# First attention pass: destination scores as a column per node tile, fetched by TensorE

## The reference

```python
h_trans = features @ W_att_w.T + W_att_b
a_src, a_dst = (a[:out_dim], a[out_dim:])
logits = leaky(h_trans[src] @ a_src + h_trans[dst] @ a_dst)
exp_l = jnp.exp(logits)
denom = jax.ops.segment_sum(exp_l, dst, num_segments=num_nodes)
alpha = exp_l / (denom[dst] + 1e-09)
h_msg = features @ W1_w.T + W1_b
h_neigh = jax.ops.segment_sum(alpha * h_msg[src], dst, num_segments=num_nodes)
```

## Time and profile before

| | us |
|---|---|
| three runs, median (lowest to highest) | 6943.19 (6922.86 to 6951.63) |
| profiled execution, span from its first to its last instruction | 5685.5 |
| busy in the span: PE, PEld | 3113.8, 2734.5 |
| busy in the span: DVE, ACT, POOL | 3263.6, 1491.5, 3958.0 |
| broadcast of 256 KB in the second pass, from issue to landing | 3.4 |

### The profile page before, as it was taken

One profiled execution on the slowest core, in us unless ns is written; L12 is line 12 of the kernel. 1 busy time (PEld: TensorE's weight loads), 2 busy tenths in 40 slices (PEclk: granted clock), 3 DMA queues, 4 the chain that ended last, 5 costly groups with the idle time before them and its releaser, 6 DMA issues. The chain is left out here.

```text
span 5685.5 us, 82572 instructions
## 1 busy us (share of the span) xinstructions
PE 3113.8 (55%) x17051; PEld 2734.5 (48%) x17052; DVE 3263.6 (57%) x12090; ACT 1491.5 (26%) x5626; POOL 3958.0 (70%) x4054
## 2 busy tenths in 40 slices
PE   4444444356666666778898988433333443333333
PEld 3333333345555555657777776333333343333332
DVE  6888887676787787744444444433444443344445
ACT  2333333345555555532222223100000000000001
POOL 3777777736777777367777772677777757777774
PEclk7555555568888777865555556666666666666666
DMA  5111112214444444222121110111111121111112
GB/s 123 52 52 52 52 52 56 49 52 131 132 132 131 130 131 131 70 54 56 52 56 51 53 52 21 56 52 51 51 51 51 51 61 52 51 51 51 51 51 57
DMA packets 222234, 385.68 MB, mean 68 GB/s; under 512 B 85452, under 2 KB 121882, under 8 KB 221998
## 3 DMA queue, kind: packets, MB, share of 16 engines
q0 software_dynamic: 142944, 296.35, 19.0%
q1 hardware_dynamic: 79054, 86.72, 5.0%
HBM read 356.23 MB, written 26.56 MB: 67 GB/s over the span
## 5 line engine op out<-in xcount | busy, mean ns | idle before, releaser
L2246 POOL DMA_INDIRECT arena<-table_gcn,idx_now x1568 | 1532.2, 977 | 642.9 <-issue 422.1
L2296 PE MATMUL pair<-arena,hotf 128*128 x3328 | 726.6, 408 | 1224.7 <-POOLq L1819 1199.3
L2296 PEld LDWEIGHTS pair<-arena,hotf 128*128 128x128 f32 x3328 | 691.2, 317 | 1256.1 <-issue 1255.8
L664 POOL DMA_INDIRECT arena<-table_attention,idx_now x832 | 825.7, 992 | 272.7 <-issue 197.2
L664 POOL DMA_INDIRECT arena<-table_key_value,idx_now x832 | 789.2, 949 | 275.9 <-issue 221.1
L1852 POOL DMA_INDIRECT arena<-table_edge_mlp,idx_now x784 | 768.1, 980 | 261.2 <-issue 212.4
L2323 DVE TENSOR_TENSOR acc<-acc,pair 128x1024 f32 x208 | 253.9, 1221 | 1133.9 <-PE pair L2299 1133.9
L1069 PE MATMUL pair<-wide,hotf 128*128 128x130 f32 x1664 | 431.0, 439 | 653.3 <-ACT wide L1033 653.3
L1069 PEld LDWEIGHTS pair<-wide,hotf 128*128 128x128 f32 x1664 | 369.0, 326 | 718.5 <-ACT wide L1033 718.5
L2256 ACT COPY idx_now<-src_t 128x8 int32 (+1 forms) x204 | 39.3, 197 | 1815.2 <-PE pair L2299 1803.2
L1406 PE MATMUL pair<-wide,hotf 128*128 128x132 f32 x1664 | 314.1, 347 | 232.9 <-DVE acc L1436 232.8
(11 more groups left out here) (371 smaller groups left out, 5709.7 us busy)
## 6 DMA issues: line engine op xcount, KB each, us to landing
key<-rel_dram SPq DMA_DIRECT2D x104, 256.0 KB, 3.4
arena<-rel_dram SPq DMA_DIRECT2D x52, 512.0 KB, 3.7
arena<-table_gcn,idx_now POOLq DMA_INDIRECT x1568, 2.5
arena<-table_attention,idx_now POOLq DMA_INDIRECT x832
arena<-table_key_value,idx_now POOLq DMA_INDIRECT x832
arena<-table_edge_mlp,idx_now POOLq DMA_INDIRECT x784, 2.4
table_attention<-arena SPq DMA_DIRECT2D x13, 512.0 KB, 3.0
table_gcn<-acc SPq DMA_DIRECT2D x26, 256.0 KB, 2.3
```

Source lines behind the costliest of these rows:

```text
L664: q_.indirect_dma_start(ring[:, slot, 0:width], None, table, bass.IndirectOffsetOnAxis(ap=idx_now[:, slot:slot + 1].bitcast(U32), axis=0)) ...
L2246: q_.indirect_dma_start(conv_ring[:, slot * D:(slot + 1) * D], None, table, bass.IndirectOffsetOnAxis(ap=idx_now[:, slot:slot + 1].bitcast ...
L2296: t_.matmul(window[:, bass.ds(offset * D, D)], hot8[:, g % 2, u, :], conv_ring[:, bass.ds(slot * D, D)], start=False, stop=False)
```

## The change

The destination scores become one column per node tile. `w0` gets the score weights as one more column, so the table's projection gives the destination score of each node in column 130, and ACT copies it into `dst_score`, 128 nodes by 52 tiles. `score` on PE, its bank and the spread copy go. At the start of the pass DVE splits the scores into three 16-bit parts (`split_scores`), whose sum is the 32-bit score.

Per group, SP's broadcasts of two groups at a time bring `rel1_dram` to all partitions; DVE makes the turned one-hot of 128x512 in 16 bits (`turned_hot`), two groups ahead; PE multiplies each step's turned one-hot with the three parts of the column of that step's node tile (`dst_scores`), one group ahead, into one column of PSUM per step. The four L938 go, and L948 reads the PSUM columns instead of `small`. SP's other writes in the pass now stand at set places between the broadcasts. In two later layers the count read from a table (`rows_of`) goes through one more register operation.

```diff
-        dst_score = look[:, :, :].rearrange("p t c -> p (t c)")
+        hotT0 = arena[:, 0:RING * G * P // 2].bitcast(BF16).rearrange("p (a e) -> p a e", a=RING)
+        rel0_rows = arena[:, RING * G * P // 2:RING * G * P].bitcast(BF16).rearrange("p (n e) -> p n e", n=2)
+        dst_score = arena[:, dst_at:dst_at + NT]
+        dst_part = arena[:, dst_at + 2 * NT:dst_at + 2 * NT + 3 * NT // 2].bitcast(BF16).rearrange("p (t c) -> p t c", c=3)
...
-                ch(v.tensor_copy(wad[:, 0:1], bank[5][:, 1:2]))
+                ch(v.tensor_copy(w0[:, D + 2:D + 3], bank[5][:, 1:2]))
...
                     if b >= 2:
                         dve.wait_ge(t0_out[b % 2], 16 * (b // 2))
+                        dve.wait_ge(score_kept, b - 1)
...
-                    t_.matmul(bank[7][:, :], wad[:, 0:1].to_broadcast([P, P]), rT[:, b % 2, :], start=True, stop=True).then_inc(score_mm, 1)
...
-                    act.wait_ge(score_mm, b + 1)
-                    s_.activation(dst_score[:, b * BT * P:(b + 1) * BT * P], bank[7][:, :], ACT.Identity, bias=wad[:, 1:2]).then_inc(score_kept, 1)
+                    act.wait_ge(t0_kept, b + 1)
+                    s_.copy(dst_score[:, b * BT:(b + 1) * BT], tT0[b % 2][:, :, D + 2]).then_inc(score_kept, 1)
...
+        dst_of = [bank[6 + n % 2][:, 0:G] for n in range(RING)]
...
                     add = back(*later(i, g, -2)) if past >= 2 else lambda u: None
-                    nodes = nodes_of(dve, regs, g)
+                    if left >= 2:
+                        turned_hot(*later(i, g, 2))
                     dve.wait_ge(l0_placed, k + 1)
                     for u in range(G):
                         v.tensor_scalar(out=hotf[:, g, u, :], ...)
                     add(0)
-                    for u in range(G):
-                        last = v.scalar_tensor_tensor(out=junk[:, 0, u * P:(u + 1) * P], in0=iota[:, :],
-                                                      scalar=rel_now[:, g * G + u:g * G + u + 1],
-                                                      in1=dst_score[:, bass.ds(nodes[u] * P, P)],
-                                                      op0=ALU.is_equal, op1=ALU.mult, accum_out=small[:, g, G + u:G + u + 1])
-                        if u == 1:
-                            add(1)
-                    ch(last)
+                    add(1)
                     add(2)
+                    dve.wait_ge(l0_dst, k + 1)
                     arrived(dve, i, g)
-                    ch.wait()
-                    ch(v.tensor_add(lg[:, g, 0, 0:G], ring[:, g * G:(g + 1) * G, D + 1], small[:, g, G:2 * G]))
+                    ch(v.tensor_add(lg[:, g, 0, 0:G], ring[:, g * G:(g + 1) * G, D + 1], dst_of[g]))
...
+                def turned_hot(i, g):
+                    k = i * RING + g
+                    dve.wait_ge(l0_rel_in[g // 2], 16 * (i + 1))
+                    if k >= RING:
+                        dve.wait_ge(l0_dst, k - RING + 1)
+                    v.tensor_scalar(out=hotT0[:, g, :], in0=rel0_rows[:, g // 2, g % 2 * G * P:(g % 2 + 1) * G * P], scalar1=part[:, 0:1],
+                                    scalar2=None, op0=ALU.is_equal).then_inc(l0_hotT, 1)
...
+                for m in range(GROUPS // 2):
+                    if m == at_pair("turned"):
...
+                    if m >= 2:
+                        sp.wait_ge(l0_hotT, 2 * m - 2)
+                    sp.dma_start(rel0_rows[:, m % 2, :], rel1_dram[m * 2 * G * P:(m + 1) * 2 * G * P].partition_broadcast(P)).then_inc(l0_rel_in[m % 2], 16)
...
+                def dst_scores(i, g):
+                    k = i * RING + g
+                    load_nodes(pe, regs, k, g)
+                    nodes = nodes_of(pe, regs, g)
+                    if k == 0:
+                        pe.wait_ge(l0_split, 5)
+                    pe.wait_ge(l0_hotT, k + 1)
+                    if k >= 2:
+                        pe.wait_ge(l0_logit, k - 1)
+                    for u in range(G):
+                        for c in range(3):
+                            last = t_.matmul(dst_of[g][:, u:u + 1], hotT0[:, g, u * P:(u + 1) * P],
+                                             flat(dst_part[:, bass.ds(nodes[u], 1), c:c + 1]), start=(c == 0), stop=(c == 2))
+                    last.then_inc(l0_dst, 1)
+
                 def step(i, g, past, left):
                     k = i * RING + g
+                    if left:
+                        dst_scores(*later(i, g, 1))
                     pe.wait_ge(l0_wide, k + 1)
...
-            eng.reg_load([need], table[0:1, bass.ds(k, 1)])
-            return eng.snap(need, min_val=0, max_val=CTILE_GROUPS - 1) + 1
+            loaded, bounded = need
+            eng.reg_load([loaded], table[0:1, bass.ds(k, 1)])
+            eng.reg_alu(bounded, loaded, 0, ALU.max)
+            return eng.snap(bounded, min_val=0, max_val=CTILE_GROUPS - 1) + 1
```

More of the change, by code:

```diff
@@ L978, in _ @@
                 load_nodes(dve, regs, 0, 0)
+                split_scores()
+                for g in range(2):
+                    turned_hot(0, g)
                 unrolled(step_and_load)
@@ L1975, in _ @@
                 slots = [dve.alloc_register(f"l2_slot{u}") for u in range(CG)]
[L1976 removed]
+                need = [dve.alloc_register(f"l2_need{n}") for n in range(2)]
                 def hot_look(i, g, k):
```

66 lines of the change are left out of this document (40 added, 26 removed).

## The result

| | before | changed |
|---|---|---|
| median of the runs, us | 6938.98 (4 runs, 6922.86 to 6951.63) | 7020.2 (4 runs, 6994.18 to 7031.01) |
| ratio | | 1.0095, 95% interval 1.0072 to 1.0117 |

A forecast was written before the change was run, and what follows sets the result against it. The prediction took POOL's gather issue pace to bound the changed pass, with DVE's work beside it. Terms -10 + 14 + 0 + 3 - 3 = +4 us gave span 5689.5; with 1257.7 held constant, 6947 us, range 6904 to 6992.

The forecast's parts named there:

- 1257.7 us lie around the span in no view; I hold them constant, although nothing shows why: Whole run: median 6943.2 us against a traced span of 5685.5; the difference was added unchanged to the forecast span.
- Cost 0: Changed pass, PE's added score matmuls: about 2.0 us a group, done 3.8 us before need, so no time lost.
- Rival three: Changed pass: PE becomes the pace above 5.2 us per group, at 0.44 us a matmul +450 us, 7400 us; chance 0.03.
- rival four: Outside the span: the time around it grows with the longer PE program; no size given; chance 0.03.
- The sum itself: All terms together: -10 + 14 + 0 + 3 - 3 = +4 us on a span of 5685.5 us.
- L938 removed (-10): Changed pass: without DVE's four L938 sums per group, POOL's issues lengthen less, between 0 and 19 us gained, -10 taken.
- the new one-hot (+14): Changed pass: DVE's 128x512 one-hot per group lengthens POOL's issues, likely ceiling 27 us, middle +14 taken.
- DMAs (+3): Changed pass: broadcasts behind SP's table writes make DVE's one-hot 2 to 5 us late at two places; 0 to +10, +3 taken.
- Ahead of the pass (-3): Batches before the pass: L594 leaves PE's chain, L634 becomes a four-column copy; between -7 and +2 us, -3 taken.
- What would show it: Profile signs: DVE busy 150 to 200 us less, landing waits up as much, PE's busy share and clock up, sorting issues 975 to 1010 ns.
- Rival one: Changed pass: POOL's issues fall to 955 ns, 36 us go and 3 ahead of the pass, 6904 us; chance 0.17.
- rival two: Changed pass: one-hot and four L934 meet a POOL issue in every group, 0.3 us each, +62, 6992 us; chance 0.15.

The follow-up runs named there:

- the unread 16-bit matmuls: Kernel before plus 17 one-column bfloat16 matmuls in each of 144 groups: 5673.57 us (1.0006); with DVE waiting for them 5664.88 us (0.9992).
- the three columns: Changed kernel with the three score parts as three columns of one matmul, 4 per group, and two more DVE additions: 5679.55 us, 1.0015.

## Why the prediction was wrong, and where it was right

**The step that failed first: "1257.7 us lie around the span in no view; I hold them constant, although nothing shows why".** Nothing of the kind exists: in every execution since, the span is 2 us shorter than the time. The trace was of an execution at the short level and the times were of the long one, so every duration, cover and wait was read from a level other than the one to be forecast. The difference between 5685.5 and 6943.2 was the one number on the page that said so; I put it into a constant.

**The step that failed by it: "Cost 0" for the wait of DVE on PE, and 0 for PE's added work.** The reason given was that the scores are done 3.8 us ahead of need. At the short level they are, by 5.7 us, and the wait is 4.8 us in the whole pass. At the long level PE's signals come some 12 us late (22.5 at the longest), more often the more instructions PE has, and no cover of 4 or 6 us holds. The chain is then: late signal, late logits, late indices from ACT, POOL idle. It goes by number of matmuls (+33, +63, +132 us for 4, 12, 24), not by their duration. The sum had no term for it. Rival three had its direction, DVE waiting for PE, but by a matmul's price, and gave it 0.03; rival four had the length of PE's program, but outside the span, where nothing is.

**The sum itself** (+4 us) came out where its rows were from: the changed kernel against before at the short level is +4.6 us (-2 to +10). Its terms, from the two traces of that level:

- *L938 removed (-10) and the new one-hot (+14)*: POOL's busy time in the pass goes from 824.9 to 823.8 us, and its mean issue while sorting is 982 ns, inside the 975 to 1010 foretold. Neither term shows, and neither can be told from nothing: the 832 issues of the pass take 811.9 to 825.7 us in the four traces of the old order at this level, and 817.2, 818.2 and 820.3 in those of the changed kernel with 12, 24 and 4 matmuls. The rule of the Trainium skill (GPSIMD Engine Reference, Key points), that GpSimd contends with DVE instructions of two SBUF inputs, would by the prediction's estimate take 10 us of stretch away with L938. The traces show no sign of it, but they differ by more than that among themselves.
- *DMAs (+3)*: right in kind and too small. The one-hot is late for its broadcast at two places, as foretold, but by 14.5 and 14.8 us and not by 2 to 5, and POOL stands behind both:

```profile
1069.67 0.35 DVE L957 TENSOR_SCALAR arena<-arena,part 128x512 bf16<-128x512 bf16 x1 [14.51 <-DMA arena<-rel_dram]
...
1071.51 0.94 POOL L662 DMA_INDIRECT arena<-table_attention,idx_now  x1 [9.09 <-DMA arena<-table_attention,idx_now]
...
1100.18 0.99 POOL L662 DMA_INDIRECT arena<-table_attention,idx_now  x1 [8.83 <-DMA arena<-table_attention,idx_now]
```

  POOL's two gaps, 4.71 and 5.08 us in the earlier trace rows, are 9.8 to 12.3 us together in the four traces of the old order and 16.1 to 18.9 us in the five with the broadcasts. That is about +6, and about all that the pass grows by from first to last issue (5.3 us, 1091.1 to 1096.4; the trace has 1095.9).
- *Ahead of the pass (-3)*: the first issue comes at 102.0 instead of 103.2 us, but at 102.6 in the earlier trace rows, and in other traces of the changed kernel at 101.3. About -1, if anything.
- *PE*: twelve matmuls take 122.4/208 = 0.59 us, not 2.0; they start within 0.55 us of each other. My 0.17 us each was over three times too much: weight load and register operation lie beside the matmul ahead, and the lower of my two prices, L1922's 0.062 us, was the near one.
- *What would show it*: DVE's busy time falls by 128 us, not by 150 to 200, and its wait for landings grows by 38 us only, with 31 for the broadcasts; PE's busy time rises by 17%, not by a third, and its clock stays (0.51 to 0.52). The span of the pass was right, 1096.4 of 1085 to 1115.

*Rival one* (POOL to its floor) and *rival two* (the one-hot meets every issue) are both out: the mean issue is neither below 960 nor above 1040 ns, and a one-hot of 8 columns changes nothing. (Rival one's price was also added up wrongly: from the pass's mean of 992 ns to 955 it is 37 ns and 31 us, not 43 and 36. And the forecast's own range, 6925 to 6970, is narrower than the ends that it was to come from, which add up to 6917 to 6982.) Of the bounded register read my 0 holds (0.9999).

What is left open: what holds an engine's instructions at the long level, what makes a series run at it, and why the loss with four matmuls is already half of that with twelve although PE is hardly held in them (DVE's one-hot, the broadcasts and the four matmuls' signals are all candidates). Neither the unread 16-bit matmuls nor the three columns ran at that level, so whether the number of PE's instructions costs by itself, or only where something waits for them, is not shown.

## What to carry to other kernels

If the span of a trace and the time of the runs differ by more than a few microseconds, the trace is of another condition than the times: say so and forecast for both, before any term is summed. Where execution can be disturbed, a cover of a few microseconds is not a cover, and work moved to an engine whose signals stand on the path cost here by the number of its instructions, not by their busy time. Before 16-bit matmuls are replaced by float32 ones in a test or a kernel, read both prices: here about 50 and 430 ns for one column.

## What the runs showed of the hardware

- The same program took about 5670 us in some series and 6940 to 7060 us in others, on one chip both within 14 minutes, and one execution of ten took 6476 us in a series that otherwise gave 5670.
- At the longer time single engines start only one instruction about every 0.7 us for several microseconds, while others go on (PE from 590.4 to 596.8 us, POOL at 1.25 us throughout), and signals of instructions that were through are recorded some 12 us later: 596.90 for a matmul started at 584.78, against 0.2 us at the shorter time.
- These holds of PE come by its instructions: one in 165 to 172 records, which is every 21 us with 12 matmuls a group and every 15 us with 24.
- A broadcast of 256 KB issued behind the write of a table of single words was awaited 14.5 and 14.8 us by DVE; elsewhere in the pass, behind no such write, not at all but for 1.5 us at its start.
- 24 one-column 16-bit matmuls a group cost nothing at the shorter time (1.0006) and 132 us at the longer.
- A one-column float32 matmul with 128x128 weights costs PE 430 ns in two pieces, one in 16 bits about 50 ns.
